# Attention maxima turned once per eight heads and carried by DMA, in a fused PixArt block on one Trainium2 core

## The reference

```python
xn = _adaln(x, noise_emb, ln1_w, ln1_b)
q, k, v = jnp.split(xn @ qkv_w.T, 3, axis=-1)      # q, k get rope, 16 heads of 32
x = x + _attn(q, k, v) @ sa_out_w.T
xn = _adaln(x, noise_emb, ln2_w, ln2_b)
q = _rope(xn @ q_w.T); k = _rope(context @ k_w.T); v = context @ v_w.T
x = x + _attn(q, k, v) @ ca_out_w.T
xn = _adaln(x, noise_emb, ln3_w, ln3_b)
x = x + (gelu(xn @ ffn_w1.T + ffn_b1) @ ffn_w2.T + ffn_b2)
# _attn: softmax(q k^T / sqrt(32)) v for each head
```

## Time and profile before

| | us |
|---|---|
| median of 3 runs | 1967.09 (1962.93 to 1968.1) |
| the profiled execution | 1963.51 |
| its span in the trace | 1961.7 |
| attention stage in it | from 0 to about 1280 |
| PE busy in the span | 1902.3 (97%) |

### The profile page before, as it was taken

One profiled execution on the slowest core, in us unless ns is written; L12 is line 12 of the kernel. 1 busy time (PEld: TensorE's weight loads), 2 busy tenths in 40 slices (PEclk: granted clock), 3 DMA queues, 4 the chain that ended last, 5 costly groups with the idle time before them and its releaser, 6 DMA issues. The chain is left out here.

```text
span 1961.7 us, 39861 instructions
## 1 busy us (share of the span) xinstructions
PE 1902.3 (97%) x13588; PEld 1653.0 (84%) x13588; DVE 1418.4 (72%) x2509; ACT 1458.3 (74%) x4005; POOL 783.0 (40%) x820
## 2 busy tenths in 40 slices
PE   7899999999999999999999998899999999999999
PEld 6688888888887888888888877678899989898998
DVE  5777778778777887887887877645666666766654
ACT  3688888888888888888888888745666565665654
POOL 4334334334334444454453442013535354454531
PEclk9899999999999999999999999999999999999999
DMA  7867776876778677778778777343322313233130
GB/s 221 221 174 196 186 188 167 202 184 170 200 201 231 166 214 216 189 202 218 184 205 217 184 206 183 94 156 108 97 92 71 108 55 114 71 97 97 54 97 33
DMA packets 300197, 307.33 MB, mean 157 GB/s; under 512 B 15840, under 2 KB 253792, under 8 KB 300000
## 3 DMA queue, kind: packets, MB, share of 16 engines
q1 hardware_dynamic: 299408, 304.45, 57.4%
q10 hardware_dynamic: 592, 0.34, 0.1%
HBM read 212.46 MB, written 92.27 MB: 155 GB/s over the span
## 5 line engine op out<-in xcount | busy, mean ns | idle before, releaser
L738 ACT ACTIVATE ps_s<-ps_s,neg_max 128x256 f32<-128x256 f32 x1024 | 459.3, 451 | 85.1 <-DVE neg_max L853 81.6
L853 DVE TENSOR_REDUCE neg_max<-ps_s 128x2 f32<-128x512 f32 x512 | 352.7, 690 | 162.7 <-PE ps_s L607 158.8
L752 ACT ACTIVATE prob<-ps_s 128x512 f32<-128x512 f32 x512 | 304.6, 595 | 61.4 <-PE ps_s L627 58.1
L923 POOL TENSOR_TENSOR rope_c<-rope_c,rope_s 128x256 f32<-128x256 f32 x128 | 98.6, 770 | 425.2 <-DVE rope_s L834 425.2
L627 PE MATMUL ps_s<-qT,kT 104*128 104x256 f32 x1024 | 213.8, 291 | 21.0 <-ACT ps_s L738 6.4
L607 PE MATMUL ps_s<-kT,qT 96*128 96x256 f32 x1024 | 218.0, 295 | 10.7 <-DMA qT<-q_turned 5.4
L597 PE MATMUL ps_g<-xx_hi,w_hi 128*128 128x256 f32 x1024 | 214.3, 291 | 7.3 <-DVE rope_s L834 3.4
L607 PEld LDWEIGHTS ps_s<-kT,qT 96*128 96x128 f32 x1024 | 172.3, 193 | 54.8 <-ACT ps_s L738 19.4
L738 ACT ACTIVATION_READ_ACCUMULATOR ps_s<-ps_s,neg_max 128x1 f32 x1024 | 213.7, 209 | 0.0
L627 PEld LDWEIGHTS ps_s<-qT,kT 104*128 104x128 f32 x1024 | 168.8, 193 | 50.6 <-issue 19.4
L597 PE MATMUL ps_g<-xx_hi,w_lo 128*128 128x256 f32 x1024 | 207.6, 285 | 0.0
(11 more groups left out here) (155 smaller groups left out, 4826.9 us busy)
## 6 DMA issues: line engine op xcount, KB each, us to landing
kT<-k_turned SPq DMA_DIRECT2D x192, 256.0 KB, 5.3
qT<-q_turned SPq DMA_DIRECT2D x64, 512.0 KB, 7.3
f_raw<-in_w1T SPq DMA_DIRECT2D x124, 256.0 KB, 3.1
k_turned<-rot_hi SPq DMA_DIRECT2D x64, 256.0 KB, 4.5
k_turned<-rot_lo SPq DMA_DIRECT2D x64, 256.0 KB, 3.0
q_turned<-rot_hi SPq DMA_DIRECT2D x64, 256.0 KB, 4.6
q_turned<-rot_lo SPq DMA_DIRECT2D x64, 256.0 KB, 3.4
qT<-q_turned SPq DMA_DIRECT2D x64, 256.0 KB, 7.8
```

What stands on the lines that cost most here:

```text
L738: ins = eng.activation(scores[:, t * L:(t + 1) * L], scores[:, t * L:(t + 1) * L], ACT.Exp, bias=neg_max[G % 2][:, t, j:j + 1], accum_out= ...
L752: eng.activation(prob[:, n % NP, :, :].rearrange("p t l -> p (t l)"), ps_s[:, score_bank(step), :], ACT.Exp).then_inc(exp_done, 1)
L853: eng.tensor_reduce(neg_max[G % 2][:, :, j], ps_s[:, score_bank(step), :].rearrange("p (t l) -> p t l", l=L), AX.X, ALU.max, negate=True). ...
L923: eng.tensor_tensor(rope_c[n % 2][:, 0, :], rope_c[n % 2][:, 0, :], rope_s[:, 0, :], ALU.subtract)
```

## The change

Five things are changed in the attention stage.

- `log`, `max_split`, `max_turn` and `max_copy` are done once for eight heads. The transpose has 16 stationary columns (eight high, eight low parts) where it had 104. ACT copies to a tile of its own, `max_rows` (two of them), and then issues two DMAs on its own queue (`max_rows`), which put the eight high rows into partition 96 of `qT` and the eight low ones into partition 97, each head's row under its head. The key stack's rows 96 and 97 hold ones. `max_spread` and the pick matrix are gone.
- LAG is 13 where it was 8, the mix comes one head sooner after a group's last `weigh` and waits for its heads by fours, the ring of weights `prob` has 9 slots for 10, and the first `weigh` of a group waits for the row DMAs.
- The stacks are loaded by four heads (`quad`), in a ring of NQ = 6, the same space: five DMAs for each four heads, where it was five for each eight.
- The projections of v are drained by DVE.
- Projections, residual loads and stores have other places.

```diff
-LAG = 8
+LAG = 13
...
-                turns(shares((p + 29, 6, k[:4]), (p + 46, 7, k[4:])))
+                turns(spread(p + 29, 13, k))
...
+                spread(*((p + 42, 9, v) if ahead == B else (p + 42, 13, v)))
             if ahead < N - 1:
-                turns(spread(p + 53, 13, q))
+                turns(spread(*((p + 42, 13, q) if ahead < B else (p + 50, 10, q) if ahead == B else (p + 29, 13, q))))
...
-            spread(p + 37, 9, [("project", "o", i - 1, t, c) for cs in (range(KC - 1), (KC - 1,)) for t in range(T) for c in cs])
-            put(p + 48, "store", i - 1)
+            put(p + 32, "res_load", i - 1)
+
+            spread(p + 55, 9, [("project", "o", i - 1, t, c) for cs in (range(KC - 1), (KC - 1,)) for t in range(T) for c in cs])
+            put(p + 66, "store", i - 1)
...
-        for half in range(2):
-            put(24 * G + 12 * half + 12, "log", G, half)
-            put(24 * G + 12 * half + 13, "max_split", G, half)
-            put(24 * G + 12 * half + 19, "max_turn", G, half)
-            put(24 * G + 12 * half + 20, "max_copy", G, half)
-            put(24 * G + 12 * half + 23, "max_spread", G, half)
-        if G:
-            put(24 * G - 20, "stack", "k", G)
-            put(24 * G - 17, "stack", "q", G)
+        for n, kind in ((24, "log"), (25, "max_split"), (30, "max_turn"), (31, "max_copy"), (32, "max_rows")):
+            put(24 * G + n, kind, G)
+    for quad in range(2, 4 * N):
+        put(12 * quad - 20, "stack", "k", quad)
+        put(12 * quad - 17, "stack", "q", quad)
 
     for G in range(2 * N):
-        place = 3 * (8 * G + LAG + 9) + 2
+        place = 3 * (8 * G + LAG + 8) + 2
...
-            NG = 3
-            qT = sb("qT", [MROWS, NG, HG, L], F32R)
-            kT = sb("kT", [MROWS, NG, HG, L], F32R)
+            NQ = 6
+            qT = sb("qT", [MROWS, NQ, OH, L], F32R)
+            kT = sb("kT", [MROWS, NQ, OH, L], F32R)
...
                     elif kind == "weigh":
                         n = step[1]
-                        G, j = divmod(n, HG)
-                        if j % OH < 2:
-                            eng.wait_ge(maxes_spread if j % OH else maxes_copied, nth["max_turn", G, j // OH])
+                        quad, j = divmod(n, OH)
+                        if n % HG == 0:
+                            G = n // HG
+                            eng.wait_ge(max_rows_in[G % 2], 16 * 2 * (G // 2 + 1))
...
                         for c in (2 * g, 2 * g + 1):
+                            eng.wait_ge(exp_done, OH * (KC * i + c + 1))
...
                     elif kind == "max_copy":
...
+                        G = step[1]
+                        eng.wait_ge(max_turned, G + 1)
+                        if G >= 2:
+                            eng.wait_ge(max_rows_in[G % 2], 16 * 2 * (G // 2))
+                        eng.activation(max_rows[G % 2][:, :], ps_s[0:2 * HG, score_bank(("max_turn", G)), 0:L],
                                        ACT.Copy).then_inc(maxes_copied, 1)
+                    elif kind == "max_rows":
+                        G = step[1]
+                        eng.wait_ge(maxes_copied, G + 1)
+                        if G >= NQ // 2:
+                            eng.wait_ge(weigh_done, HG * (G - NQ // 2 + 1))
+                        first = 2 * G % NQ
+                        for s in range(2):
+                            into = qT[ROWS + s:ROWS + s + 1, first:first + 2, :, :]
+                            eng.dma_start(into.rearrange("p g h l -> p (g h) l").bitcast(F32),
+                                          max_rows[G % 2][s * HG:(s + 1) * HG, :].bitcast(F32)).then_inc(max_rows_in[G % 2], 16)
...
-                    elif kind == "max_spread":
-                        G, half = step[1:]
-                        eng.wait_ge(maxes_copied, nth[step])
-                        rows = qT[ROWS:MROWS, G % NG, OH * half:OH * (half + 1), :]
-                        eng.tensor_copy(rows[:, 1:OH, :], rows[:, 0:1, :].broadcast_to([2 * OH, OH - 1, L])).then_inc(maxes_spread, 1)
```

More of the change, by code:

```diff
@@ L97, in stage_order @@
                 put(p + late + place, *step)
-            x_place = p + late + (31 if ahead == B else 16)
+            x_place = p + late + (31 if ahead == B else 18 if B < ahead < N else 16)
             for half in range(2):
@@ L165, in stage_order @@
     yield ("warm", WARM_START)
-    yield ("pick",)
+    yield ("ones",)
     for h in range(2):
@@ L217, in stage_order @@
     yield from rotated("q", 0)
-    yield ("stack", "k", 0)
+    for quad in range(2):
+        yield ("stack", "k", quad)
     yield from (step for step in early if step[0] in turns_of_x)
@@ L221, in stage_order @@
     yield from rotated("k", 1)
-    yield ("stack", "q", 0)
+    for quad in range(2):
+        yield ("stack", "q", quad)
     yield from split("v", range(KC), "o")
@@ L384, in block_kernel @@
             total = [sb(f"total{n}", [P, T, HG]) for n in range(2)]
-            log_sb = [sb(f"log_sb{n}", [P, T, OH]) for n in range(2)]
-            shift = sb("shift", [P, T, OH])
-            max_parts = sb("max_parts", [P, T, MROWS])
-            NP = 10
+            log_sb = sb("log_sb", [P, T, HG])
+            shift = sb("shift", [P, T, HG])
+            max_parts = sb("max_parts", [P, T, ROWS])
+            max_rows = [sb(f"max_rows{n}", [2 * HG, L], F32R) for n in range(2)]
+            NP = 9
             prob = sb("prob", [P, NP, T, L])
@@ L412, in block_kernel @@
             spilled = {m: [sem(f"spilled_{m}{t}") for t in range(T)] for m in "qk"}
-            stack_in = {m: [sem(f"stack_{m}{n}") for n in range(2)] for m in "qk"}
+            stack_in = {m: [sem(f"stack_{m}{n}") for n in range(4)] for m in "qk"}
+            max_rows_in = [sem(f"max_rows_in{n}") for n in range(2)]
             STACKS = {"q": 2, "k": 3}
@@ L708, in attention_scalar @@
                             eng.activation(ctx_hi[:, ks, :], xT[:, ks, :], ACT.Copy).then_inc(ctx_hi_done, 1)
-                    elif kind == "project" and step[1] == "v" and step[4] == KC - 1:
-                        i, t = step[2:4]
-                        eng.wait_ge(product_done, products["v", i, t])
-                        if i >= NV and t == 0:
-                            eng.wait_ge(mix_done, KC * (i - NV + 1))
-                        eng.activation(v_sb[i % NV][:, t, :], ps_g[:, bank(("project", "v", i, t, 0)), :],
-                                       ACT.Copy).then_inc(v_done, 1)
                     elif kind == "rope_high":
@@ L741, in attention_scalar @@
                     elif kind == "log":
-                        G, half = step[1:]
-                        eng.wait_ge(total_done, HG * G + OH * (half + 1))
-                        if nth[step] > 2:
-                            eng.wait_ge(shift_done, nth[step] - 2)
-                        eng.activation(log_sb[half][:, :, :], total[G % 2][:, :, OH * half:OH * (half + 1)], ACT.Ln).then_inc(log_done, 1)
+                        G = step[1]
+                        eng.wait_ge(total_done, HG * (G + 1))
+                        if G:
+                            eng.wait_ge(shift_done, G)
+                        eng.activation(log_sb[:, :, :], total[G % 2][:, :, :], ACT.Ln).then_inc(log_done, 1)
                     elif kind == "weigh":
@@ L812, in attention_vector @@
                                           ALU.subtract).then_inc(w_split, 1)
-                    elif kind == "pick":
-                        eng.wait_ge(small_in["pick"], 2 * 16)
-                        for r in range(NG):
-                            for half in range(2):
-                                eng.tensor_copy(kT[ROWS:MROWS, r, OH * half:OH * (half + 1), :],
-                                                pick_sb[ROWS:MROWS, :].unsqueeze(2).broadcast_to([2 * OH, OH, L])).then_inc(picked, 1)
+                    elif kind == "ones":
+                        eng.memset(kT[ROWS:MROWS, :, :, :].bitcast(F32), 1.0).then_inc(ones_set, 1)
                     elif kind == "project" and step[1] in "qk" and step[4] == KC - 1:
@@ L835, in attention_vector @@
                                           ALU.mult).then_inc(rope_taken, 1)
+                    elif kind == "project" and step[1] == "v" and step[4] == KC - 1:
+                        i, t = step[2:4]
+                        eng.wait_ge(product_done, products["v", i, t])
+                        if i >= NV and t == 0:
+                            eng.wait_ge(mix_done, KC * (i - NV + 1))
+                        eng.tensor_copy(v_sb[i % NV][:, t, :], ps_g[:, bank(("project", "v", i, t, 0)), :]).then_inc(v_done, 1)
                     elif kind == "project" and step[1] == "o" and step[4] == KC - 1:
```

115 lines of the change are left out of this document (49 added, 66 removed).

## The result

| | before | after |
|---|---|---|
| median, us | 1967.59 (4 runs) | 1946.74 (1945.83 to 1949.51, 4 runs) |
| the profiled execution | 1963.51 | 1946.9 |
| its span | 1961.7 | 1945.1 |

The ratio is 0.9899, 95% interval [0.9879, 0.992]: 1.0% faster, 20.9 us by the medians and 16.6 by the profiled executions. Forecast were 13 us by the sum. The direction is right and the time lies in the range, but the sum came out near by two errors that cancel in part, as the experiments show.

What follows compares the result with a forecast made beforehand. The prediction took PE's work to bound the attention stage's middle (94% of an item). Terms -9.0 - 9.6 - 1.4 + 10 - 3 gave -13 us from 1963.5, or 1950.5; the median, 3.6 above, was forecast at 1954 us, range 1930 to 1996.

Steps and rivals of the forecast that it cites:

- Turns, -9.0: On PE in the attention stage, 64 of 128 turns go at 0.14 us each: -9.0 us.
- Waits for the copied and spread rows, -9.6: `weigh` on PE no longer waits for DVE's spread (5.6 us) or ACT's copy (4.0): -9.6 us.
- for v's drain, -1.4: PE's one wait for the drain of v, at the change of layers, goes: -1.4 us.
- the rival "nothing": Waits return for the next in line, only the turns and little else are gained: 1963 us, chance 0.22.
- "Give nothing by themselves.": The spread's 121.4 us on DVE and the halved copies and logarithms lay beside PE's work: no gain by themselves.
- Row DMAs, +10: PE waits 0.3 us for the row DMAs in each of 32 even groups, landing taken as 2.7 us: +10 us.
- The rival "late rows": Row DMAs land later than 3.1 us, making the kernel slower: 1995 us at 4.0, 2062 at 5.3; chance 0.27.
- Second pass, mix and drain, 0 with 4 either way: Longer lag and closer mix stay hidden, the longer drain is offset before it: 0, with 4 us either way.
- Stacks, 0: Stack loads by four heads add ten issues per item on SP, some 6 us, hidden: 0.
- Clock, -3: Fewer waits at the ends and change of layers recover a sixth of 19.2 us lost to low clock: -3 us.

Runs made afterwards that it cites:

- the two edits: Kernel before the change, with DVE's 128 spread copies left out and v's drain moved from ACT to DVE: 1946.06 us, ratio 0.9898.
- the last version: Changed kernel with the last statistics of x later and DVE's scaling of x behind the split: 1943.43 us, ratio 0.9872.

## Why the prediction was right, and where it was not

Its sum was -13 us against the profiled execution, which moved by 16.6. The account below is of that pair of executions; by the ratio the gain is 19.9.

*Turns, -9.0.* Mis-sized: -13.8 (64 x 0.215). The mechanism was right, and the version with the turns done twice shows the size, within 11 to 16 us. Nothing is visible for the fewer columns: the start behind a turn of 16 columns comes after 0.14 us as behind one of 104.

*Waits for the copied and spread rows, -9.6, and for v's drain, -1.4.* The rows are gone. In the second layer the copy's wait was worth 0.51 an item, not 0.28. But other waits of PE came, for the split above all (14.5 us), so the rival "nothing" was right that waits come back as waits for the next in line.

*"Give nothing by themselves."* This step failed. The spread's 121 us on DVE and v's 38 on ACT (64 x 0.6), both beside PE's work, were worth 18 us together; 119 us of idle work given to DVE in the changed kernel take its gain away. The argument "PE's own work is 94% of the item, so the others' time is free" fails on the other 6%. Of these 2.2 us half was PE's work not counted (x's transposes, turns at their full price: after, an item with two turns and no waits takes 35.7, so one with four 36.1). The other half, 1.1 us of 37.2, was waits of a few tenths at fixed places, set by how late ACT and DVE are, and it is what the two edits won: 9.9 us in nine items, in the three places shown above. In the second layer, where they are in time (36.6 us an item with and without the two edits), the claim holds.

*Row DMAs, +10.* The size fits (8.1 us recorded) by luck, for the form does not. Forecast were tenths in each of 32 even groups; found were seven waits of 0.2 to 2.2 us, six in even groups and one in an odd, at the start, in four items of the first layer, at the change of layers and at the end, none in the second layer's middle. The chain was shorter than 3.0 us before the second issue. ACT of after behind the turn at 831.61:

```profile
832.76 0.36 ACT L713 ACTIVATE max_rows<-ps_s 16x256 fp32r<-16x256 f32 x1
833.02 0.41 ACT L733 ACTIVATE ps_s<-ps_s,neg_max 128x256 f32<-128x256 f32 x1
833.14 0.66 ACTq L723 DMA_DIRECT2D qT<-max_rows  x1
...
833.47 0.41 ACT L733 ACTIVATE ps_s<-ps_s,neg_max 128x256 f32<-128x256 f32 x1
833.83 0.18 ACT L733 ACTIVATION_READ_ACCUMULATOR ps_s<-ps_s,neg_max 128x1 f32 x1
833.83 0.64 ACTq L723 DMA_DIRECT2D qT<-max_rows  x1
```

The copy starts 1.15 us after the turn, not 1.74 (in the first layer's odd groups 1.88). The first issue begins at the copy's end and does not wait for the second activation, though both stand ahead of it in the queue. The second follows 2.22 us after the turn. The `weigh` starts at 836.82, 5.21 after it, as forecast (5.2 to 5.4). So a landing up to 3.0 us is hidden, not up to 2.4, and in 18 even groups of the version with LAG at 12 it took 2.05 to 2.11. The Trainium skill ("DMA: Bandwidth & Descriptors", Anatomy of one DMA) gives a fixed 2.0 us, in a section on DMAs that GpSimd issues; these are ScalarE's. The shortest landings agree with it, the others of that version took 2.2 to 4.8, and the seven waits of after imply 2.9 to 4.8. The rival "late rows" was right that landings over 3.1 us come, and wrong on where: in the second layer of that version they fall in odd groups, where the `weigh` comes 4.8 us behind the second issue. With one head less of lag it is the result, 2016 us.

*Second pass, mix and drain, 0 with 4 either way.* The drain grew by 8.0 us and the stretch before it shrank by 4.3: +3.7, inside. *Stacks, 0.* Before, scores waited for a stack of q for 5.4 us in three places, 3.4 of it at head 0 and 2.0 behind 1220 us, a row that the prediction did not count; after, no such row is left. Head 0 starts 2.4 us later all the same, behind more projection work placed ahead of it. The landings are shorter than in the earlier trace rows, of stack loads of half the size:

```profile
kT<-k_turned SPq DMA_DIRECT2D x384, 128.0 KB, 3.0
...
k_turned<-rot_lo SPq DMA_DIRECT2D x64, 256.0 KB, 2.7
```

*Clock, -3.* 70 x 0.12 + 40 x 0.09 + 120 x 0.04 = 16.8 us against 19.2: -2.4.

*What the sum lacked.* Turns 13.8 and the two engines' relief 18.2 are 32.0 us; 16.6 came. So 15.4 were given back. The table has 15.2 of them, after against "no spread, v on DVE" with 0.43 us an item taken off for the halved turns: 9.0 us in the nine items to head 192, 6.7 at the change of layers, 5.4 from head 448 to the end of the stage, 1.0 before head 48; against that the second layer won 6.9 more, of which 6.1 are the copy's waits (12 x 0.51). The scatter of 1 to 3 us in a stretch lies on each of these. In the first layer the turn's wait for the split (0.6 us an item from start to start) and the row DMAs are seen in these places. But the last version shows that the split's waits were hardly a cost of their own: without them ACT's came. Counted from the other end the excess is the same, but it is shared out otherwise: in the changed kernel the spread's time is worth 20.7 us by the spans, the turns 13.0 and v's drain 1.1, together 34.8. So what one part is worth depends on which others are in place. What the change of layers lost was not taken apart by a run; there PE's starts come late by 4.3 us for ACT in two places and by 2.3 for the row DMAs.

So two errors of opposite sign cancelled in part: a gain not foreseen (18.2 where 11.0 of waits were booked, turns 4.8 short: 12.0), and 15.4 given back where 10 for the row DMAs were booked and 3 credited for the clock (8.4 more). That leaves 3.6 of the 16.6 above the forecast 13, about what one execution differs from the next by; that the sum came so near is luck.

## What to carry over

Before calling an engine's time free because another is 97% busy, look for waits that recur once per item: give the engine idle work, or take work off it, and time that. Price an instruction from the start of its predecessor to where the old cadence is back, since part of it can stand behind the next row; a wait likewise. And a wait that a table names is not a gain until the next in line (here ACT's exp at the score bank) has been looked at: 5.9 us of them, taken away in two ways, made the kernel 7 to 9 us slower and changed about nothing.

## What the runs showed of the hardware

- A DMA issue on ACT's queue ran while activations ahead of it in program order were still to finish: issue at 833.14, the second activation ahead of it at 833.47. An issue took 0.63 to 0.66 us there, where it was 0.34 to 0.43 at the start.
- With LAG at 12, an 8 KB DMA from SBUF to SBUF landed 2.05 to 4.8 us after its issue began. The 18 landings up to 2.11 all follow 4 us in which SyncE issued at most one DMA; 18 of the 19 over 3 us follow 4 us with four to six.
- Two 128-column transposes cost about 0.215 us in a stream of matmuls: 0.14 until the next start and 0.08 more on the pair behind. A mix does the same: the pair of scores behind it held 0.34 us before the next start (422.73, has a modelled time of 0.50 where others have 0.40).
- After a listed wait of 0.28 us the next start came 0.44 late, and after one of 0.32 us 0.47 late (345.25, behind a 512-column matmul at 344.54 that holds 0.24). The pair behind took 0.07 and 0.10 more.
- The same 13588 instructions of PE were busy for 1902.3 us in the kernel before and for 1887.3 with both edits: a modelled busy time holds waits that no row lists, and time at the lower clock (granted clock 0.990 and 0.994 over the run).
